# Two attention layers and an MLP on one core: loads, additions and one statistics operation placed in other slots

## The chip, the cores and the metric

The kernel runs on one core of a Trainium2 chip. The metric is the device time of one execution in microseconds (us), the median of several runs. Five engines work side by side: TensorE (PE, matmuls; its weight loads are PEld), VectorE (DVE), ScalarE (ACT), GpSimd (POOL) and SyncE (SP). SP computes nothing here; it issues DMAs, and ACT issues some too. Each engine runs its own list of instructions in the order in which the program wrote them, and waits at semaphores for the others.

## The reference, cut to what matters

The input x holds 16 batches of 256 tokens of 512 numbers; `ctx` has the same shape. All is float32, with 16 heads of 32.

```
ln = layernorm(x, ln1); q, k, v = split(ln @ w_qkv + b_qkv)
x = x + attention(q, k, v, ltor_mask) @ w_ao + b_ao          # first layer
ln = layernorm(x, ln2); q = ln @ w_q + b_q
k, v = split(ctx @ w_kv + b_kv)
x = x + attention(q, k, v, cross_mask) @ w_co + b_co         # second layer
x = x + gelu(layernorm(x, ln3) @ w1 + b1) @ w2 + b2          # MLP
# then a block of three small 1x1 convolutions of x and ctx, and their products, added to x

attention: scores = q k^T / sqrt(32); scores = scores * mask - 10000 * (1 - mask)
           softmax over the last axis, then times v
```

The products run in split precision: an operand is written as a high and a low part (names that end in `_h` and `_l`), and a product is three matmuls (lines L66, L67 and L68).

## The kernel before, in words

**Bodies and slots.** Two batches (512 tokens, four tiles of 128) are one block. The two attention layers are 16 bodies, k = 0 to 15: bodies 0 to 7 are the first layer over the eight blocks, bodies 8 to 15 the second. In a body the kernel works on block r and lets the work of its neighbours overlap: it prepares x and the contexts of the next block, and finishes the output product of the block before (k - 1). Each body has eight slots, h = 0 to 7. Each slot handles one group of four heads of one batch at each stage of a pipeline: the scores of one group, the maxima and exponentials of the group before it, the turns (transposes) and the product with v of a still older one. In the same slot TensorE has two units of a projection: q and k in slots 0 to 3, v in slots 4 and 6, and in slots 5 and 7 the output product of the block before, whose tiles are o0, o1 (slot 5) and o2, o3 (slot 7).

**What a slot needs from each engine.** TensorE: the units (L66 to L68), the scores (L1052), the product with v (L1086), the turns (L1068). VectorE: the masked scores (L1655, 128x1024, two of them, called mask here), the row maxima (L1665, eight, each with two inputs in SBUF), the low part of q or k (L1638), or for an output tile the sum of the product in PSUM and the residual (L1633); then the reciprocals (L1672) and their transpose (L1675), and the scaling of the product with v (L1693). ScalarE: exponentials (L1306), copies of the turned exponentials (L1367), the high parts. GpSimd: the low part of the weighed product (L817), the halves of the contexts (L805, L810), and the addition of the output bias to each residual tile (`add_bias`, L776, two SBUF inputs, 128x512).

**Two trips through DRAM.** The reciprocals go from `A_turned_inv` to `inverses` in DRAM and come back as `A_rt` (issued by SP, L533 and L543), and VectorE needs them at L1693. The exponentials go out (L555) and come back turned as `A_pt` (L565), which TensorE needs at L1086.

**Residual tiles.** The tile buffers `res[0]` and `res[1]` serve o0, o1 and then o2, o3. Tile t is loaded from `x` (function `load_res` of ScalarE's queue, slot 2 for tiles 0 and 1, slot 6 for tiles 2 and 3), gets its bias from GpSimd (slot 4; slot 7), is added to the product by VectorE (slot 5; slot 7), and is stored by SP (`store`, L503).

**Other work that the change touches.** `chunks` are pieces of the second layer's weights (128x512), loaded into `wst` by SP in bodies 7 and 8 (`load_chunk`, L490) and split into high and low part by the other engines (`split_chunk`). The loads of the contexts of the next block are in ScalarE's queue. `row_statistics` (VectorE, L1603) takes the batch statistics of a tile of x for the next layer norm: two tiles in slot 0, two in slot 1. In body 15 GpSimd also normalises rows for the MLP (L909 to L914).

The order on every engine is the order in which the program writes it: nothing is planned at run time. Where an instruction waits, all behind it on that engine wait too.

Of the kernel before, what the change touches and what calls it, by code (L numbers as in the profile page):

```python
# [11 lines left out]
P = 128  # L12
# [125 lines left out]
def whole_network(nc, ctx, nl, m1t_dram, inv_dram, p_dram, xt_dram, rows, x1, x2, ctx_t, s_mask, x_mask, s_weights, x_weights, fold_wt, columns,  # L138
# [20 lines left out]
    KEPT = range(GROUPS - 12, GROUPS)  # L159

    with ExitStack() as stack:
# [150 lines left out]
        chunk_at = {(7, 4): (0, 1, 2), (7, 5): (3, 4), (7, 6): (5,), (7, 7): (6, 7)}  # L312
        chunk_at.update({(8, 0): (8,), (8, 1): (9,), (8, 2): (10, 11)})
        chunk_at.update({(9, n): (12 + n,) for n in range(4)})
        load_at = {(7, 0): (0, 1), (7, 3): (2, 3), (7, 4): (4, 5), (7, 6): (6, 7), (7, 7): (8,), (8, 0): (9,), (8, 1): (10, 11),
# [14 lines left out]
        ld_x, ld_e = room.sems("ld_x", TT), room.sems("ld_e", BPB)  # L330
        ld_r, st_y, ld_m = room.sems("ld_r", 2), room.sems("st_y", 2), room.sems("ld_m", BPB)
# [149 lines left out]
        def _(sp):  # L481
            def load_chunk(n):
                c, t = chunks[n]
                if n < KT:
                    sp.wait_ge(folded, 4 * KT)
                elif chunks[n - KT][0] == 0:
                    sp.wait_ge(w_lo, 4 * KT + chunks[n - KT][1] + 1)
                else:
                    sp.wait_ge(w_lo2, sum(1 for c_, _ in chunks[:n - KT + 1] if c_))
                sp.dma_start(wst[:, n % KT, :], x_weights[c][t * P:(t + 1) * P, :]).then_inc(ld_s[n % KT], DMA)  # L490
# [131 lines left out]
            def slot(r, k, h, a_, b_, own, pv):  # L622
# [135 lines left out]
        def _(pool):  # L758
# [94 lines left out]
            def slot(r, k, h, a_, b_, own, pv):  # L853
# [3 lines left out]
                if h == 7 and k < NU:  # L857
                    if k:
# [18 lines left out]
                if h == (4 if 1 < k < NU else 1) and k:  # L877
# [381 lines left out]
        def _(act):  # L1259
# [303 lines left out]
        def _(dve):  # L1563
# [60 lines left out]
            def unit_out(item, r, k):  # L1624
# [148 lines left out]
            def slot(r, k, h, a_, b_, own, pv):  # L1773
# [40 lines left out]
                if k < NU and h in ((0, 1) if k else (1, 2)):  # L1814
                    row_statistics(r + 1, 0 if h == (0 if k else 1) else 2)
# [189 lines left out]
```

## Time and profile before

| | |
|---|---|
| median of three runs | 2012.24 us (2012.05 to 2014.52) |
| the profiled execution | 2015.01 us |
| its span in the trace | 2013.2 us |
| TensorE busy | 1976.3 us (98%) |
| VectorE busy | 1476.2 us (73%) |
| ScalarE busy | 1161.6 us (58%) |
| GpSimd busy | 547.1 us (27%) |
| granted TensorE clock | 0.998 of full speed |

Bodies 0 to 15 end at about 1235 us of the span, and the rest is MLP and the last block, which the change doesn't touch. The page says "busy" for a matmul with a modelled end, so a gap on TensorE looks a little shorter than the delay it stands for. A row of a timeline is: start, duration, engine, line, operation, tiles, count; in square brackets how long the engine had been idle before, and who released it. The waits view sums these gaps by line and by releaser.

### The profile page before, as it was taken

How to read it: one execution, taken by the hardware profiler on the slowest of the kernel's cores; microseconds unless marked ns; L12 is line 12 of the kernel's file. 1: busy time of each engine (PE TensorE's matmuls, PEld its weight loads, DVE VectorE, ACT ScalarE, POOL GpSimd, SP SyncE). 2: the span in 40 equal slices, each digit the busy share in tenths (PEclk: the TensorE clock that was granted, in tenths of full speed). 3: DMA queues.
4: the chain of work that ended last, by engine and by line, in shares of the span. 5: the costliest groups of instructions: out<-in, count | busy, mean ns of one | idle time of the engine just before them, and what ended most of it. 6: DMA issues, size and time to landing. Idle time of an engine off the chain costs nothing. (4 is left out here: it accounts for less than half of the span.)

```text
span 2013.2 us, 41550 instructions
## 1 busy us (share of the span) xinstructions
PE 1976.3 (98%) x13632; PEld 1569.7 (78%) x13632; DVE 1476.2 (73%) x3868; ACT 1161.6 (58%) x3251; POOL 547.1 (27%) x556
## 2 busy tenths in 40 slices
PE   9999999999999999999999998999999999999998
PEld 8977777777776777777777776888888888888887
DVE  7799999999998999899899889564444443435333
ACT  4388888888888888888888888521212111212111
POOL 1012222222224334323423432053132131313000
PEclk9999999999999999999999999999999999999999
DMA  8546667667667877767867734541212212121201
GB/s 273 173 94 139 147 165 158 129 162 163 135 176 184 194 171 171 172 160 172 184 150 166 187 92 116 171 107 35 79 40 69 68 47 78 47 63 51 62 24 48
DMA packets 681720, 252.67 MB, mean 126 GB/s; under 512 B 533312, under 2 KB 626112, under 8 KB 681536
## 3 DMA queue, kind: packets, MB, share of 16 engines
q1 hardware_dynamic: 533600, 192.16, 38.1%
q10 hardware_dynamic: 147936, 58.22, 12.0%
q8 instruction: 95, 1.56, 0.3%
q14 instruction: 89, 0.73, 0.1%
HBM read 167.41 MB, written 82.84 MB: 124 GB/s over the span
## 5 line engine op out<-in xcount | busy, mean ns | idle before, releaser
L1306 ACT ACTIVATE A_p<-A_p,A_nmax 128x256 f32<-128x256 f32 x1024 | 507.1, 501 | 3.5 <-DVE A_res L1633 1.7
L1665 DVE CUSTOM_DVE_ANT_0 A_p<-A_p,A_ma 128x256 f32<-128x256 f32 x1024 | 377.1, 423 | 4.6
L1655 DVE TENSOR_TENSOR A_p<-A_sc,A_mk 128x1024 f32<-128x1024 f32 x256 | 312.1, 1219 | 50.8 <-PE A_tp L1068 50.2
L817 POOL TENSOR_TENSOR A_ct_l<-A_cx,A_ct_h 128x256 fp32r<-128x256 f32 x122 | 114.2, 936 | 653.0 <-DVE A_nmax L1665 639.5
L1367 ACT ACTIVATE A_pt<-A_tp 128x512 f32<-128x512 f32 x396 | 218.2, 588 | 51.4 <-PE A_tp L1068 50.2
L1068 PEld LDWEIGHTS A_tp<-A_ident,A_p 128*128 128x128 f32 x1584 | 179.4, 141 | 72.6 <-ACT A_p L1306 35.4
L1068 PE MATMUL A_tp<-A_ident,A_p 128*128 128x128 f32 x1584 | 223.1, 278 | 2.9 <-ACT A_pt L1367 2.1
L1504 ACT ACTIVATE A_mk<-A_tp,A_cols 128x512 f32<-128x512 f32 x62 | 42.7, 689 | 269.0 <-PE A_tp L68 269.0
L1306 ACT ACTIVATION_READ_ACCUMULATOR A_p<-A_p,A_nmax 128x1 f32 x1024 | 197.4, 193 | 0.0
L1504 ACT ACTIVATE A_ma<-A_tp,A_cols 128x512 f32<-128x512 f32 x62 | 42.8, 690 | 242.1 <-PE A_tp L68 242.1
L66 PE MATMUL A_banks<-A_xt_h,A_w_h 128*128 128x512 f32 x384 | 162.0, 422 | 3.3 <-DVE A_res L1633 2.3
L1856 DVE CAST A_h_h<-A_ma 128x512 fp32r<-128x512 f32 x64 | 33.5, 524 | 161.8 <-ACT A_ma L1504 158.1
L68 PE MATMUL A_banks<-A_xt_h,A_w_l 128*128 128x512 f32 x384 | 151.1, 394 | 0.0
L926 POOL TENSOR_TENSOR A_v<-A_v,A_b_row 128x512 f32<-128x512 f32 x32 | 51.3, 1624 | 365.2 <-DMA A_v<-x 365.2
L67 PE MATMUL A_banks<-A_xt_l,A_w_h 128*128 128x512 f32 x384 | 150.2, 391 | 0.0
L1374 ACT ACTIVATE A_cx<-A_cx,A_bias_sum 128x256 f32<-128x256 f32 x128 | 65.2, 509 | 140.4 <-DVE A_cx L1693 140.2
L66 PE MATMUL A_tp<-A_xt_h,A_w_h 128*128 128x512 f32 x368 | 143.4, 390 | 0.3 <-DVE A_xt_l L1870 0.3
L67 PE MATMUL A_tp<-A_xt_l,A_w_h 128*128 128x512 f32 x368 | 143.2, 389 | 0.0
L68 PE MATMUL A_tp<-A_xt_h,A_w_l 128*128 128x512 f32 x368 | 143.2, 389 | 0.0
L1086 PE MATMUL A_banks<-A_pt,A_v 128*32 128x256 f32 x2048 | 137.9, 387 | 4.5 <-DMA A_pt<-exponentials 2.2
L1856 DVE CAST A_h_h<-A_mk 128x512 fp32r<-128x512 f32 x64 | 30.0, 468 | 143.0 <-ACT A_mk L1504 140.8
L66 PE MATMUL A_banks<-A_w_h,A_ct_h 128*128 128x512 f32 x256 | 105.9, 414 | 1.6 <-issue 1.1
(248 smaller groups left out, 4997.2 us busy)
## 6 DMA issues: line engine op xcount, KB each, us to landing
exponentials<-A_ln_shift SPq DMA_DIRECT2D x464, 64.0 KB, 2.7
A_pt<-exponentials SPq DMA_DIRECT2D x116, 256.0 KB, 3.1
A_rt<-inverses SPq DMA_DIRECT2D x512, 32.0 KB, 2.6
x<-A_res SPq DMA_DIRECT2D x64, 256.0 KB, 3.6
A_res<-x ACTq DMA_DIRECT2D x58, 256.0 KB, 4.3
turned<-A_x ACTq DMA_DIRECT2D x224, 64.0 KB, 2.7
A_x<-x ACTq DMA_DIRECT2D x56, 256.0 KB, 3.3
A_x<-x SPq DMA_DIRECT2D x40, 256.0 KB, 3.2
```

Of the source, the lines that this page charges most:

```text
L66: pe.matmul(out, sh, mh, start=first, stop=False)
L67: pe.matmul(out, sh, ml, start=False, stop=False)
L68: return pe.matmul(out, sl, mh, start=False, stop=last)
L817: pool.tensor_tensor(ct_l[:, f, part], cx[:, :], f32(ct_h[:, f, part]), ALU.subtract).then_inc(c_lo, 1)
L1068: last = pe.transpose(tp[:, n % 2, c * S + t * P:c * S + (t + 1) * P], p[:, g % 2, j, t, c * P:(c + 1) * P], ident[:, :])
L1086: last = pe.matmul(banks[rr, bank, 0:S], v[:, b * TPB + c, f * P + j * HD:f * P + (j + 1) * HD], turned_keys(grp, j, c), start=(c == 0), s ...
L1306: act.activation(p[:, g % 2, j, t, :], p[:, g % 2, j, t, :], ACT.Exp, scale=-1.0, bias=nmax[:, g % 2, j, t:t + 1], accum_out=rsum[:, g % 2 ...
L1367: act.activation(pt[:, moved(grp) + i, :, :], tp[:, n % 2, :].rearrange("p (c s) -> p c s", c=TPB), ACT.Copy)\
L1374: act.activation(cx[:, :], cx[:, :], ACT.Identity, bias=bias_sum[:, layer(k, h, -2), 2, f:f + 1]).then_inc(c_sum, 1)
L1504: act.activation(hf[f % 4], hidden_bank(blk, f), ACT.Gelu_apprx_tanh, bias=b1_col[:, f:f + 1])\
L1655: dve.tensor_tensor(p[:, g % 2, heads, :, :].rearrange("p j t s -> p j (t s)"), sc[:, heads, :], m, ALU.mult)\
L1665: dve.tensor_tensor_reduce(out=a_, in0=a_, in1=ma[:, b, t, :], scale=-1.0, scalar=BIG, op0=ALU.add, op1=ALU.min, accum_out=nmax[:, g % 2, ...
```

## The change

Five edits, none of which changes what is computed.

1. **Contexts.** For the bodies 8 to 14 the loads of the next block's two contexts (512 KB each) move on ScalarE's queue from slots 2 and 3 to slots 1 and 2. Body 7 has them there already.
2. **Body 15's first additions.** Residual tiles 0 and 1 are loaded in slot 0 in place of slot 2, and GpSimd adds their bias in slot 1 in place of slot 4.
3. **Chunks.** In body 7 the loads of chunks 4 and 5 move on SP from slot 4 to slot 5, and chunk 4 is split in slot 6 with chunk 5, no longer in slot 5 with chunk 3.
4. **A statistics operation.** The statistics of tile 0 move from slot 0 to the end of slot 7 of the body before, behind the sum for o3. So that its x is there, the load of this tile moves from ScalarE's queue (slot 6) to SP's (slot 5).
5. **Two more residual tiles.** In the bodies of `FOUR` (4, 5, 6, 10, 11, 12, 13) tiles 2 and 3 live in `wst[2]` and `wst[3]`, which are free there. They are loaded on ScalarE's queue in slot 3 in place of slot 6, and GpSimd adds both biases in slot 5 in place of slot 7.

```
-        chunk_at = {(7, 4): (0, 1, 2), (7, 5): (3, 4), (7, 6): (5,), (7, 7): (6, 7)}
+        chunk_at = {(7, 4): (0, 1, 2), (7, 5): (3,), (7, 6): (4, 5), (7, 7): (6, 7)}
-        load_at = {(7, 0): (0, 1), (7, 3): (2, 3), (7, 4): (4, 5), (7, 6): (6, 7), ...
+        load_at = {(7, 0): (0, 1), (7, 3): (2, 3), (7, 5): (4, 5), (7, 6): (6, 7), ...
+        def res_tile(k, t):
+            return wst[:, t, :] if four(k, t) else res[:, t % 2, :]
+        def four(k, t):
+            return k + 1 in FOUR and t > 1
...
 SP, load_chunk:
+                    for half_ in range(2):
+                        sp.wait_ge(st_y[half_], (7 - 1) * 2 * DMA)
 SP, slot:
+                if by_blocks(k) and h == 5:
+                    sp.wait_ge(st_a[0], (turned_before(k, r) + 1) * TPB * (P // 32) * DMA)
+                    sp.dma_start(x[:, 0, :], row_tile(0, k + 2, r + 2, 0)).then_inc(ld_x[0], DMA)
...
 GpSimd, slot:
                 if h == 7 and k < NU:
-                    if k:
+                    if k and k not in FOUR:
                         add_bias(k - 1, r - 1, 2)
                         until_first_maxima(r, h)
                         add_bias(k - 1, r - 1, 3)
-                if h == (4 if 1 < k < NU else 1) and k:
+                if h == (4 if 1 < k < NU - 1 else 1) and k:
                     add_bias(k - 1, r - 1, 0)
                     add_bias(k - 1, r - 1, 1)
+                if h == 5 and k in FOUR:
+                    add_bias(k - 1, r - 1, 2)
+                    add_bias(k - 1, r - 1, 3)
...
 ScalarE, loads:
-                if by_blocks(k) and (h, n) == (6, 3):
-                    load_row(k + 2, r + 2, 0)
-                if NB <= k + 1 < NU and n == 4 and h in ((1, 2) if k + 1 == NB else (2, 3)):
-                    load_context(r + 1, h - (1 if k + 1 == NB else 2))
+                if NB <= k + 1 < NU and n == 4 and h in (1, 2):
+                    load_context(r + 1, h - 1)
-                if 1 < k < NU and h == 2 and n in (5, 6):
+                if 1 < k < NU and h == (2 if k < NU - 1 else 0) and n in (5, 6):
                     load_res(k - 1, r - 1, n - 5)
-                if 0 < k < NU and h == 6 and n in (5, 6):
-                    load_res(k - 1, r - 1, n - 3)
+                if 0 < k < NU and h == (3 if k in FOUR else 6) and n in ((3, 4) if k in FOUR else (5, 6)):
+                    load_res(k - 1, r - 1, n - (1 if k in FOUR else 3))
...
 VectorE, slot:
-                    row_statistics(r + 1, 0 if h == (0 if k else 1) else 2)
+                    if h != 0 or k < 2:
+                        row_statistics(r + 1, 0 if h == (0 if k else 1) else 2)
...
+                if by_blocks(k) and h == 7:
+                    row_statistics(r + 2, 0)
```

TensorE's own list of instructions stays as it is. Three places of the lists that change are shown here; the names are those of the tiles, written `output<-inputs`.

GpSimd, body 10, slots 4 to 7, before. `A_et_h` and `A_et_l` are the two parts of a context, `A_ct_l` is the low part of the weighed product, which waits for the maxima of its slot:

```order
L776 TENSOR_TENSOR A_res<-A_res,A_o_bias 128x512 x2
L817 TENSOR_TENSOR A_ct_l<-A_cx,A_ct_h 128x256
L805 CAST A_et_h<-A_e 128x4x128
L810 TENSOR_TENSOR A_et_l<-A_e,A_et_h 128x4x128
L805 CAST A_et_h<-A_e 128x4x128
L810 TENSOR_TENSOR A_et_l<-A_e,A_et_h 128x4x128
L805 CAST A_et_h<-A_e 128x4x128
L817 TENSOR_TENSOR A_ct_l<-A_cx,A_ct_h 128x256
L810 TENSOR_TENSOR A_et_l<-A_e,A_et_h 128x4x128
L776 TENSOR_TENSOR A_res<-A_res,A_o_bias 128x512 x2
```

The same place after:

```order
L797 TENSOR_TENSOR A_res<-A_res,A_o_bias 128x512 x2
L838 TENSOR_TENSOR A_ct_l<-A_cx,A_ct_h 128x256
L826 CAST A_et_h<-A_e 128x4x128
L831 TENSOR_TENSOR A_et_l<-A_e,A_et_h 128x4x128
L826 CAST A_et_h<-A_e 128x4x128
L831 TENSOR_TENSOR A_et_l<-A_e,A_et_h 128x4x128
L797 TENSOR_TENSOR A_wst<-A_wst,A_o_bias 128x512 x2
L826 CAST A_et_h<-A_e 128x4x128
L838 TENSOR_TENSOR A_ct_l<-A_cx,A_ct_h 128x256
L831 TENSOR_TENSOR A_et_l<-A_e,A_et_h 128x4x128
```

These rows (with the renumbered lines L817 to L838, L805 to L826, L810 to L831) show that the second pair of additions has moved from behind the third context half to directly behind the second.

SP, body 7, slots 4 to 6, before:

```order
L490 DMA A_wst<-L_xattn_w_q 128x512
L490 DMA A_wst<-L_xattn_w_kv 128x512
L565 DMA A_pt<-exponentials 128x4x128
L533 DMA inverses<-A_turned_inv 128x32
L555 DMA exponentials<-A_ln_shift 32x16x32 x4
L543 DMA A_rt<-inverses 32x4x64 x4
L731 DMA A_e<-turned 128x4x256
L503 DMA x<-A_res 128x512 x2
```

The same place after:

```order
L583 DMA A_pt<-exponentials 128x4x128
L551 DMA inverses<-A_turned_inv 128x32
L573 DMA exponentials<-A_ln_shift 32x16x32 x4
L561 DMA A_rt<-inverses 32x4x64 x4
L752 DMA A_e<-turned 128x4x256
L508 DMA A_wst<-L_xattn_w_q 128x512
L508 DMA A_wst<-L_xattn_w_kv 128x512
L687 DMA A_x<-x 128x512
L521 DMA x<-A_res 128x512 x2
```

The two chunk loads went from ahead of the slot's trips through DRAM to behind them, and the load of x's tile 0 stands behind them, ahead of the stores; this last load stands at that place in bodies 1 to 14.

The third place is on VectorE, at the end of slot 7 and in slot 0 of the next body. Before, in slot 0, both statistics stand in front of the low part of k:

```order
L1665 ISA A_nmax 128x1
L1603 BN_STATS A_stats<-A_x 128x6 x2
L1638 SCALAR_TENSOR_TENSOR A_k_l<-A_banks,A_bias_sum,A_k_h 128x512
L1655 TENSOR_TENSOR A_p<-A_sc,A_mk 128x1024
L1672 RECIPROCAL A_rinv<-A_rsum 128x8
```

After, from the end of the body before:

```order
L1644 TENSOR_TENSOR A_xt_l<-A_e,A_xt_h 128x4x256
L1655 TENSOR_TENSOR A_res<-A_banks,A_res 128x512
L1625 BN_STATS A_stats<-A_x 128x6
L1677 TENSOR_TENSOR A_p<-A_sc,A_mk 128x1024
L1694 RECIPROCAL A_rinv<-A_rsum 128x8
```

and in slot 0 itself:

```order
L1687 ISA A_nmax 128x1
L1625 BN_STATS A_stats<-A_x 128x6
L1660 SCALAR_TENSOR_TENSOR A_k_l<-A_banks,A_bias_sum,A_k_h 128x512
L1677 TENSOR_TENSOR A_p<-A_sc,A_mk 128x1024
L1694 RECIPROCAL A_rinv<-A_rsum 128x8
```

One of the two statistics stands in front of the low part of k where two stood, and the other stands ahead of the body's first mask.

## Rows read from the trace of the kernel before

**Rows 1.** The page: busy us of each engine, share, instructions.

```profile
PE 1976.3 (98%) x13632; PEld 1569.7 (78%) x13632; DVE 1476.2 (73%) x3868; ACT 1161.6 (58%) x3251; POOL 547.1 (27%) x556
```

**Rows 2.** Waits of TensorE, 140 to 651 us: total, times, longest.

```profile
PE A_banks L1086 <- DMA A_pt<-exponentials: 2.2, 3, 1.3
PE A_banks L66 <- DVE A_res L1633: 1.4, 4, 0.5
```

**Rows 3.** Waits of TensorE, 651 to 1161 us.

```profile
PE A_banks L66 <- DVE A_k_l L1638: 5.1, 8, 0.8
PE A_banks L66 <- DVE A_res L1633: 0.8, 3, 0.5
```

**Rows 4.** Timeline, VectorE and TensorE, body 9, slot 3.

```profile
748.15 0.42 DVE L1693 TENSOR_TENSOR A_cx<-A_banks,A_rt 128x256 f32<-128x256 f32 x1 [0.98 <-DMA A_rt<-inverses]
...
751.82 0.39 PE L1052 MATMUL A_sc<-A_k_h,A_q_h 32*128 32x256 f32 x4
...
752.74 1.07 PE L1086 MATMUL A_banks<-A_pt,A_v 128*32 128x256 f32 x16
...
755.62 0.50 PE L66 MATMUL A_banks<-A_w_h,A_et_h 128*128 128x512 f32 x1 [0.79 <-DVE A_k_l L1638]
```

**Rows 5.** Timeline, VectorE and TensorE, slot 7 of body 5 and what follows it.

```profile
488.11 0.42 DVE L1693 TENSOR_TENSOR A_cx<-A_banks,A_rt 128x256 f32<-128x256 f32 x1 [0.77 <-DMA A_rt<-inverses]
...
495.42 0.50 PE L66 MATMUL A_banks<-A_xt_h,A_w_h 128*128 128x512 f32 x1 [0.53 <-DVE A_res L1633]
```

**Rows 6.** Timeline, VectorE and TensorE, slot 0 of bodies 7 and 8.

```profile
574.72 1.29 DVE L1603 BATCH_NORM_STATS2 A_stats<-A_x 128x6 f32<-128x512 f32 x2
...
576.71 0.50 PE L66 MATMUL A_banks<-A_xt_h,A_w_h 128*128 128x512 f32 x1 [0.35 <-DVE A_k_l L1638]
...
655.06 0.50 PE L66 MATMUL A_banks<-A_xt_h,A_w_h 128*128 128x512 f32 x1 [0.55 <-DVE A_k_l L1638]
```

**Rows 7.** Timeline, SP's queue and TensorE, body 7, slots 4 and 5.

```profile
613.11 0.35 SPq L490 DMA_DIRECT2D A_wst<-L_xattn_w_q  x1
617.90 0.35 SPq L490 DMA_DIRECT2D A_wst<-L_xattn_w_kv  x1
618.35 0.38 SPq L565 DMA_DIRECT2D A_pt<-exponentials  x1
...
622.75 1.94 PE L1086 MATMUL A_banks<-A_pt,A_v 128*32 128x256 f32 x16 [1.29 <-DMA A_pt<-exponentials]
```

**Rows 8.** Timeline, body 15: GpSimd in its slot 4, VectorE and TensorE in slot 5.

```profile
1200.60 2.98 POOL L776 TENSOR_TENSOR A_res<-A_res,A_o_bias 128x512 f32<-128x512 f32 x2
...
1204.41 1.38 POOL L912 TENSOR_TENSOR A_x<-A_x,A_o_bias 128x512 f32<-128x512 f32 x1
...
1204.57 1.51 DVE L1665 CUSTOM_DVE_ANT_0 A_p<-A_p,A_ma 128x256 f32<-128x256 f32 x1
...
1209.15 0.39 PE L1052 MATMUL A_sc<-A_k_h,A_q_h 32*128 32x256 f32 x4 [0.92 <-DVE A_p L1655]
...
1213.04 0.50 PE L66 MATMUL A_banks<-A_w_h,A_et_h 128*128 128x512 f32 x1 [0.89 <-DVE A_res L1633]
```

**Rows 9.** Timeline, body 10: GpSimd in its slot 5, VectorE and TensorE in slot 6.

```profile
848.21 1.29 POOL L810 TENSOR_TENSOR A_et_l<-A_e,A_et_h 128x512 fp32r<-128x512 f32 x1
...
849.15 0.64 DVE L1665 CUSTOM_DVE_ANT_0 A_p<-A_p,A_ma 128x256 f32<-128x256 f32 x1
...
849.72 0.41 DVE L1665 CUSTOM_DVE_ANT_0 A_p<-A_p,A_ma 128x256 f32<-128x256 f32 x1
...
850.76 1.21 DVE L1655 TENSOR_TENSOR A_p<-A_sc,A_mk 128x1024 f32<-128x1024 f32 x1
...
852.82 0.39 PE L1052 MATMUL A_sc<-A_k_h,A_q_h 32*128 32x256 f32 x4
...
855.58 0.48 PE L66 MATMUL A_banks<-A_w_h,A_ct_h 128*128 128x512 f32 x1
```

**Rows 10.** Windows, body 9, slots 5 and 6: busy us by engine, clock, DMA share, GB/s.

```profile
772.60:778.60 6.00, 6.00 (x37) 5.09 (x34) 5.13 (x14) 4.26 (x11) 4.12 (x5) 1.00 1.01 254
```

More of the change, by code:

```diff
@@ L159, in whole_network @@
     KEPT = range(GROUPS - 12, GROUPS)
+    FOUR = (4, 5, 6, 10, 11, 12, 13)
     with ExitStack() as stack:
@@ L311, in whole_network @@
         chunks = [(0, 0), (1, 0), (0, 1), (0, 2), (0, 3), (1, 1), (1, 2), (1, 3)] + [(2, t) for t in range(KT)] + [(3, t) for t in range(KT)]
-        chunk_at = {(7, 4): (0, 1, 2), (7, 5): (3, 4), (7, 6): (5,), (7, 7): (6, 7)}
+        chunk_at = {(7, 4): (0, 1, 2), (7, 5): (3,), (7, 6): (4, 5), (7, 7): (6, 7)}
         chunk_at.update({(8, 0): (8,), (8, 1): (9,), (8, 2): (10, 11)})
         chunk_at.update({(9, n): (12 + n,) for n in range(4)})
-        load_at = {(7, 0): (0, 1), (7, 3): (2, 3), (7, 4): (4, 5), (7, 6): (6, 7), (7, 7): (8,), (8, 0): (9,), (8, 1): (10, 11),
+        load_at = {(7, 0): (0, 1), (7, 3): (2, 3), (7, 5): (4, 5), (7, 6): (6, 7), (7, 7): (8,), (8, 0): (9,), (8, 1): (10, 11),
                    (8, 2): (12,), (8, 3): (13, 14, 15)}
@@ L330, in whole_network @@
         ld_x, ld_e = room.sems("ld_x", TT), room.sems("ld_e", BPB)
+        ld_r4 = room.sems("ld_r4_", 2)
         ld_r, st_y, ld_m = room.sems("ld_r", 2), room.sems("st_y", 2), room.sems("ld_m", BPB)
@@ L431, in raw_pair, with res_loaded @@
             return e[:, n, :, :] if k < NB else f32(xt_l[:, :, 2 * n * P:(2 * n + 2) * P])
+        def res_tile(k, t):
+            return wst[:, t, :] if four(k, t) else res[:, t % 2, :]
+        def four(k, t):
+            return k + 1 in FOUR and t > 1
+        def res_loaded(k, t):
+            if four(k, t):
+                return ld_r4[t % 2], sum(four(m, t) for m in range(k + 1)) * DMA
+            return ld_r[t % 2], (sum(2 - four(m, 2) for m in range(k)) + t // 2 + 1) * DMA
         def late(k, h):
@@ L498, in load_res @@
                 wait(sp, st_y[t % 2], (r * 2 + t // 2) * DMA)
-                sp.dma_start(res[:, t % 2, :], row_tile(0, k, r, t)).then_inc(ld_r[t % 2], DMA)
+                sp.dma_start(res[:, t % 2, :], row_tile(0, k, r, t)).then_inc(res_loaded(k, t)[0], DMA)
             def store(k, r, t):
                 sp.wait_ge(y_ok, r * TT + (t + 1))
-                sp.dma_start(row_tile(1, k, r, t), res[:, t % 2, :]).then_inc(st_y[t % 2], DMA)
+                sp.dma_start(row_tile(1, k, r, t), res_tile(k, t)).then_inc(st_y[t % 2], DMA)
             def load_m_chunk(n):
@@ L774, in add_bias @@
             def add_bias(k, r, t):
-                pool.wait_ge(ld_r[t % 2], (r * 2 + (t // 2 + 1)) * DMA)
-                pool.tensor_tensor(res[:, t % 2, :], res[:, t % 2, :], o_bias[:, int(k >= NB), :], ALU.add)\
+                pool.wait_ge(*res_loaded(k, t))
+                pool.tensor_tensor(res_tile(k, t), res_tile(k, t), o_bias[:, int(k >= NB), :], ALU.add)\
                     .then_inc(res_ok, 1)
@@ L1326, in load_res @@
             def load_res(k, r, t):
-                wait(act, st_y[t % 2], (r * 2 + t // 2) * DMA)
-                act.dma_start(res[:, t % 2, :], row_tile(0, k, r, t)).then_inc(ld_r[t % 2], DMA)
+                wait(act, st_y[t % 2], (r * 2 + (0 if four(k, t) else t // 2)) * DMA)
+                act.dma_start(res_tile(k, t), row_tile(0, k, r, t)).then_inc(res_loaded(k, t)[0], DMA)
             def load_o_copy(t):
@@ L1632, in unit_out @@
                     dve.wait_ge(res_ok, (r - 1) * TT + (n + 1))
-                    dve.tensor_tensor(res[:, n % 2, :], o, res[:, n % 2, :], ALU.add).then_inc(y_ok, 1)
+                    dve.tensor_tensor(res_tile(k - 1, n), o, res_tile(k - 1, n), ALU.add).then_inc(y_ok, 1)
                 else:
```

## The prediction

> **What bounds the kernel now.** I read four views in this order. The page first: TensorE is busy 98% of the span [rows 1], so a move can only give back the few per cent of gaps in TensorE's row, or open new ones. Then TensorE's waits for the two attention layers [rows 2, 3]: they are a handful of small items, each with its releaser. Then the timeline at each item, upstream from TensorE to the engine that was late and to what made it late [rows 4 to 9]. Last a window for the DMA engines [rows 10].
>
> How a gap becomes time: in a slot without a wait, the next unit's first matmul starts 855.58 - 852.82 = 2.76 us after the scores [rows 9]. In body 9 it is 755.62 - 751.82 = 3.80, so the delay is 1.04 where the bracket says 0.79 [rows 4]. I add 0.25 to each recorded gap. A body that waits nowhere takes about 8 slots of one length, so a delay on TensorE goes into the end one for one; nothing later makes it up.
>
> **The change part by part (gain positive).**
>
> *Body 7, chunks.* SP issues the load of chunk 4 at 613.11, then stands before chunk 5 until 617.90, which holds the load of `A_pt` behind it until 618.35. TensorE waits 1.29 for it, and the 16 small matmuls then take 1.94 in place of 1.07 [rows 7, 4]. With both chunk loads a slot later, behind that load, the sum is 1.29 + 0.25 + 0.87 = 2.4. Chunk 4's split moves beside chunk 5's, which could take some of it back: between 0.5 and 2.7. I take 2.4, as the wait is seen whole.
>
> *Statistics.* In slot 0 of bodies 7 and 8 the two operations take 1.29 ahead of the low part of k, and TensorE then waits 0.35 and 0.55 [rows 6]; as delays 0.60 and 0.80. One operation less there is 0.65: gain 0.6 + 0.65 = 1.2. The other bodies have room for it in slot 0. At the end of slot 7 it stands behind the sum for o3, so it can delay only the next mask. Bounds -0.5 to 1.4.
>
> *Body 15.* GpSimd's two residual additions in slot 4 push the row additions L912 and its successor to 1204.41, where VectorE's maxima run: one takes 1.51 [rows 8] where another takes 0.41 [rows 9], and the next one is met in the same way. TensorE then waits 0.92 for the mask and 0.89 for o1's sum [rows 8]: 1.17 + 1.14 = 2.3. In slot 1 the additions fall on work that they don't block, if their loads land in time; I take 2.1, bounds 1.0 and 2.3.
>
> The Trainium skill (SBUF — State Buffer, "Who interferes with whom") states that a VectorE instruction with two SBUF inputs and a GpSimd instruction that reads SBUF lock each other out for a whole instruction. By that rule the maximum waits for the addition's end, and the trace agrees (1.51 against 0.41).
>
> *Slot 7, layer 1.* `A_rt` comes late there: VectorE idles 0.77 for it in body 5 and TensorE 0.53 at the end [rows 5]. Four such waits are 1.4 recorded [rows 2], 2.4 as delays. Bodies 4 to 6 lose two tile loads and the x load from slot 6, bodies 1 to 3 the x load alone. I take all of body 5 but a little (0.7), a third of the other three (0.6), and 0.2 off for new loads in slot 3: 1.1, bounds 0 and 2.4.
>
> *Slot 7, layer 2, bodies 10 to 13.* Three waits of 0.8 together [rows 3] are 1.55 as delays, and a fourth body has some 0.3 below the resolution of that view. All four lose three loads from slot 6: gain 1.9, bounds 0.5 and 1.9.
>
> *The same bodies, the additions in slot 5.* This is the costly term. In layer 1 the two additions of slot 5 follow the weighed product at once and are over before the maxima begin. In bodies 10 to 13 two context splits come first. The second ends at 848.21 + 1.29 = 849.50, and the first maximum, begun at 849.15, takes 0.64 since it is held until then [rows 9]. Now two additions of 1.3 each follow directly, over the maxima at 849.72 and behind it. As in body 15, each addition holds one maximum for 1.51 - 0.41 = 1.1. The mask that followed at 850.76 and ended at 851.97 comes 2.2 later, and the scores at 852.82 have 0.85 of room [rows 9]: a delay of 1.35 in slot 6. Four bodies: -5.4. Bounds: 0 (the additions slip between the maxima, which the 0.64 of the first one would allow) and 4 x 2.2 = 8.8 (the room is used up by something else). I take 5.4, as rows 8 show the same pair of operations.
>
> *Contexts.* One slot earlier they run beside x's tile load, two slots later beside two residual loads as before. In slot 3 of bodies 8 to 14 TensorE waits for k's low part, because `A_rt` comes 0.98 late behind one context and two residual tiles [rows 4]; eight waits of 5.1 are listed [rows 3]. The second context stays in slot 2 with both tiles, so these stay. Slot 1 takes 0.75 MB in place of slot 2's 1.0 MB, so I expect the trip there to be just in time: -0.5 for all seven bodies, bounds 0 and 7 x 1.04 = -7.3.
>
> *The x load on SP* stands behind the slot's trips through DRAM and ahead of two stores of the same size; nothing waits for these soon. In the slots 5 and 6 the DMA engines are full, 1.01 at 254 GB/s [rows 10], and the next `A_pt` and `inverses` are queued behind. I take -0.3 for it in all, with a rival below.
>
> The Trainium skill (DMA: Bandwidth & Descriptors, "Issuing engines are not separate DMA queues") says that DMAs started by different engines run on the same 16 and interleave. By it, moving x's load from ScalarE's queue to SP's saves no transfer time: what this term gives must come from the slot alone. Rows 10 show the crowd but not the origin of each packet.
>
> Sum: 2.4 + 1.2 + 2.1 + 1.1 + 1.9 - 5.4 - 0.5 - 0.3 = 2.5. The profiled execution took 2015.01 us, 2.8 above the median of 2012.24; the terms are differences and hold for either. Median: 2009.7, profiled execution about 2012.5.
>
> **The rivals.**
>
> *No collision.* The additions fall between the maxima, or the mask's room takes them up: 5.4 comes back, 2004.3. For it: the first maximum loses 0.23 only today [rows 9]. Against: additions back to back leave no gap, and rows 8 have two maxima held in a row.
>
> *Slower by the contexts.* If the context in slot 1 makes `A_rt` as late as in rows 4, slot 2 of bodies 8 to 14 gets a delay of 1.04 each: -7.3 in place of -0.5, 2016.5. It decides from the point where the trip lands more than about 0.4 after VectorE asks for it. For it: rows 4. Against: a quarter less to move than there, and body 7 has its contexts so placed and lists no such wait of its own in rows 2.
>
> *Slower by x's load.* At 254 GB/s its 256 KB are 1.03 us of full engines [rows 10]. If that falls on the trip for slot 7, the seven bodies with a wait there (4 + 3 in rows 2, 3) lose 1.03 each and the other seven half of it: 10.8. Without the two gains of slot 7 (3.0) and the -0.3: 2009.7 + 3.0 - 0.3 + 10.8 = 2023.2. Against it: the same 256 KB leave slot 6 at once, and in seven bodies 512 KB more.
>
> *Body 7 only shifts its stall.* The splits of chunks 4 and 5 together delay the mask of slot 6 as the missing load did: 1.9 less, 2011.6.
>
> **How the numbers follow.** A measurement of this kernel can tell about 0.2%, 4.0 us, from no change: faster is below 2008.2, slower above 2016.3. Chances: the forecast 0.56, with its own range 2006.5 to 2012.5, and 0.30 of it below 2008.2; no collision 0.20, nearly all faster; contexts 0.09, somewhat over half slower; x's load 0.05, slower; body 7 0.10, same. That gives faster 0.17 + 0.19 = 0.36, slower 0.05 + 0.05 + 0.01 = 0.11, same 0.53. The range leaves out the lower part of "no collision", x's load and the worse half of the contexts: 2002.8 to 2015.0.
>
> **What would show it.** In the changed kernel: in slot 6 of bodies 10 to 13 two maxima of some 1.5 us beside the `A_wst` additions, and a gap on TensorE before the scores, released by VectorE's mask, about 1.1 recorded. If these maxima stay near 0.4, the costly term is wrong. In body 7 no SP wait before `A_pt` and no gap before its product; if a gap before the scores of slot 6 or 7 of the same size is there, the stall has moved. The waits on `A_res` at the bodies' ends gone for 5 and 10 to 13, smaller for 1 to 3. Body 15 without its two gaps. The eight waits for k's low part after slot 3 still there, those of bodies 7 and 8 after slot 0 gone. New gaps after slot 2 in bodies 8 to 14, or `A_rt` waits on VectorE in slots 6 and 7, would speak for the slower rivals.

## The result, and the profile after

| | before | after |
|---|---|---|
| median (12 runs each) | 2012.14 us | 2017.26 us |
| range | 2007.87 to 2014.52 | 2014.00 to 2019.77 |
| ratio | | 1.0027, 95% interval 1.0020 to 1.0034 |
| profiled execution | 2015.01 us | 2018.07 us |
| span | 2013.2 us | 2016.2 us |

The change made the kernel slower by 0.27%, some 5.4 us, where 2.5 us of gain was forecast. The time lies outside the forecast's range. VectorE's busy time rose by 5.6 us, though it runs the same operations; the page of the changed kernel [rows 1 before]:

```profile
span 2016.2 us, 41547 instructions
PE 1977.5 (98%) x13632; PEld 1570.7 (78%) x13632; DVE 1481.8 (73%) x3868; ACT 1161.6 (58%) x3251; POOL 550.1 (27%) x556
```

TensorE's waits from 651 to 1161 us, the stretch of [rows 3], as total, times and longest:

```profile
PE A_sc L1076 <- DVE A_p L1677: 7.5, 5, 1.9
PE A_banks L66 <- DVE A_k_l L1660: 2.2, 5, 0.7
PE A_banks L66 <- DVE A_res L1655: 0.2, 1, 0.2
```

The waits on `A_res` at the ends of the bodies shrank as forecast. In their place TensorE waits for VectorE's mask (L1677, L1655 before): four waits of 1.8 to 1.9 us and a small one. Body 10, in the order GpSimd, VectorE, TensorE; it answers to [rows 9] (columns: start, duration, engine, line, operation):

```profile
845.09 1.29 POOL L831 TENSOR_TENSOR A_et_l<-A_e,A_et_h 128x512 fp32r<-128x512 f32 x1
846.33 2.93 POOL L797 TENSOR_TENSOR A_wst<-A_wst,A_o_bias 128x512 f32<-128x512 f32 x2
849.20 0.81 POOL L826 CAST A_et_h<-A_e 128x512 fp32r<-128x512 f32 x1
...
846.02 0.64 DVE L1687 CUSTOM_DVE_ANT_0 A_p<-A_p,A_ma 128x256 f32<-128x256 f32 x1
...
846.59 1.51 DVE L1687 CUSTOM_DVE_ANT_0 A_p<-A_p,A_ma 128x256 f32<-128x256 f32 x1
...
848.03 1.51 DVE L1687 CUSTOM_DVE_ANT_0 A_p<-A_p,A_ma 128x256 f32<-128x256 f32 x1
...
849.47 0.82 DVE L1687 CUSTOM_DVE_ANT_0 A_p<-A_p,A_ma 128x256 f32<-128x256 f32 x1
...
850.22 1.21 DVE L1677 TENSOR_TENSOR A_p<-A_sc,A_mk 128x1024 f32<-128x1024 f32 x1
...
851.58 0.39 PE L1076 MATMUL A_sc<-A_k_h,A_q_h 32*128 32x256 f32 x4 [1.82 <-DVE A_p L1677]
```

All four maxima are held: the first by the split (0.64, as before), two by the additions, and the fourth by the cast that follows them. The mask starts 4.20 us after the first maximum, where it was 850.76 - 849.15 = 1.61 before [rows 9]: 2.6 us more. The room before the scores takes 0.7 of it.

A second thing stands behind the gap. After it the product with v and the turns take their usual time in body 11, and nearly twice that in body 12. TensorE's timeline, body 12:

```profile
1000.75 1.91 PE L1110 MATMUL A_banks<-A_pt,A_v 128*32 128x256 f32 x16
1002.59 1.87 PE L1092 MATMUL A_tp<-A_ident,A_p 128*128 128x128 f32 x8
```

and body 11:

```profile
926.90 1.07 PE L1110 MATMUL A_banks<-A_pt,A_v 128*32 128x256 f32 x16
927.90 1.09 PE L1092 MATMUL A_tp<-A_ident,A_p 128*128 128x128 f32 x8
```

The windows view of the same two places (columns: busy us of the five engines, granted clock, DMA share, GB/s):

```profile
1001.00:1004.30 3.30, 3.30 (x25) 2.13 (x17) 1.90 (x4) 0.60 (x2) 2.86 (x3) 0.51 0.59 187
927.00:930.00 3.00, 3.00 (x30) 2.20 (x31) 2.91 (x7) 1.29 (x4) 2.41 (x2) 1.00 0.73 191
```

In body 12 the granted clock was 0.51, the lower of the two levels (1.2 GHz), right after an idle time of 1.83 us. I call this the half clock; it costs 1.62 us more. In this trace it happened in bodies 12 and 13 and not in 10 and 11, though all four gaps were 1.82 to 1.85 us.

In body 7 the wait for `A_pt` moved. SP's queue and TensorE in slots 5 and 6, to be read beside [rows 7]:

```profile
622.85 0.50 SPq L508 DMA_DIRECT2D A_wst<-L_xattn_w_q  x1
623.40 0.43 SPq L508 DMA_DIRECT2D A_wst<-L_xattn_w_kv  x1
623.87 0.43 SPq L687 DMA_DIRECT2D A_x<-x  x1
624.34 0.92 SPq L521 DMA_DIRECT2D x<-A_res  x2
625.66 0.37 SPq L583 DMA_DIRECT2D A_pt<-exponentials  x1
...
633.30 1.07 PE L1110 MATMUL A_banks<-A_pt,A_v 128*32 128x256 f32 x16 [1.97 <-DMA A_pt<-exponentials]
```

Five transfers of 256 KB stand ahead of it, and TensorE waits 1.97 us for it, here with no half clock behind it (the 16 matmuls take 1.07). Body 15 has neither of its gaps any more ([rows 8]; between 1161 and 1232 us the waits view lists nothing).

**Where the 3.1 us between the two spans are.** I compared the distance from each slot's scores to the next in both traces. What a distance has above that of a slot without a wait (8.9 us) is called the slot's delay.

| place | change, us | forecast |
|---|---|---|
| bodies 10 to 13, delay before the scores of slot 6 | +7.6 (4 x 1.90) | +5.4 |
| bodies 12 and 13, half clock behind it | +3.2 | none |
| bodies 10 to 13, slot 7 | -1.65 | -1.9 |
| body 7, slots 5 to 7 | -1.4 (-2.80 and +1.41) | -2.4 |
| bodies 7 and 8, slot 0 | -1.1 | -1.2 |
| body 15 | -1.9 | -2.1 |
| bodies 1 to 6, slots 6 and 7 | +1.2 | -1.1 |
| bodies 8 to 14, slots 2 and 3 | -3.8 | +0.5 |
| rest (bodies 8, 9, 14 and small ones) | +0.9 | +0.3 |

The eighth row is no effect of the change. These two slots have 7.4 us of delay in the profiled execution before and 3.6 to 5.1 in each of the 17 other traces of this study, also where nothing of them was edited. That execution was 2.9 us above its own median. A term of one or two us read from one execution has this much luck in it.

The fourth row has luck in it too. The 2.80 us of slot 5 hold a stretch at half clock behind the wait of 1.29 us [rows 7]. In s1, s2 and s4 (below), where edit 3 is absent too, the same wait is 1.02 to 1.11 us, the matmuls behind it take their usual time, and the delay of the slot is 1.1 to 1.2. From s1:

```profile
621.54 1.07 PE L1086 MATMUL A_banks<-A_pt,A_v 128*32 128x256 f32 x16 [1.09 <-DMA A_pt<-exponentials]
```

Slots 5 and 6 of body 7 have to be read together, since these traces have a wait of 1.70 to 1.86 us in slot 6: their delay is 3.4 before, 2.9 in s1, 3.0 in s4, 4.5 in s2 with half clock, 1.0 in s3 and 2.0 in the changed kernel.

### The profile page after: what moved, and what is told of

The parts are those of the page before. It is cut to its first block and busy times, and to the rows that moved or that the text cites. A ratio compares the mean times of both kernels' runs of the same rounds, so it can differ in the third digit from the quotient of the medians.

```text
span 2016.2 us, 41547 instructions
## 1 busy us (share of the span) xinstructions
PE 1977.5 (98%) x13632; PEld 1570.7 (78%) x13632; DVE 1481.8 (73%) x3868; ACT 1161.6 (58%) x3251; POOL 550.1 (27%) x556
## 5 line engine op out<-in xcount | busy, mean ns | idle before, releaser
L1687 DVE CUSTOM_DVE_ANT_0 A_p<-A_p,A_ma 128x256 f32<-128x256 f32 x1024 | 385.3, 431 | 4.6
L1677 DVE TENSOR_TENSOR A_p<-A_sc,A_mk 128x1024 f32<-128x1024 f32 x256 | 312.1, 1219 | 49.8 <-PE A_tp L1092 48.1
L838 POOL TENSOR_TENSOR A_ct_l<-A_cx,A_ct_h 128x256 fp32r<-128x256 f32 x122 | 114.4, 938 | 681.1 <-DVE A_nmax L1687 667.6
```

The costliest lines, as they stand in the source:

```text
L838: pool.tensor_tensor(ct_l[:, f, part], cx[:, :], f32(ct_h[:, f, part]), ALU.subtract).then_inc(c_lo, 1)
L1677: dve.tensor_tensor(p[:, g % 2, heads, :, :].rearrange("p j t s -> p j (t s)"), sc[:, heads, :], m, ALU.mult)\
L1687: dve.tensor_tensor_reduce(out=a_, in0=a_, in1=ma[:, b, t, :], scale=-1.0, scalar=BIG, op0=ALU.add, op1=ALU.min, accum_out=nmax[:, g % 2, ...
```

## The experiments

All ratios are to the kernel before on the same chip. The first eight ran beside a kernel before of 2011.4 and 2011.6 us. Three theories stood at the start: A, VectorE's maxima and GpSimd's instructions exclude each other, and the clock falls behind the gap; B, the transfers moved in SP's queue and into other slots cost the time everywhere; D, GpSimd's writes or the late context half behind the additions, not the reads, are at fault.

**The additions of bodies 10 to 13.**

e1, only bodies 4, 5 and 6 keep their tiles 2 and 3 in `wst`:

```
-    FOUR = (4, 5, 6, 10, 11, 12, 13)
+    FOUR = (4, 5, 6)
```

> The changed kernel with FOUR = (4, 5, 6): the bodies 10 to 13 load and add their residual tiles 2 and 3 as before, in slots 6 and 7. Theory A (shared port, then clock): the four delays of 1.90 us before the scores of slot 6 go, 7.6 us, and with them the two stretches of 1.62 us at half clock behind them, 3.2 us; the waits at the ends of these bodies come back, 1.7 us. From 2017.3: 2008.2, and about 0.2% below the kernel before. Rival B (the x load in SP's queue and the additional traffic in slots 5 and 6 cost the time everywhere): at most a quarter of the loss goes, 2015 to 2017.

Measured: 2007.47 us, ratio 0.9981 (0.9972 to 0.9990). As theory A expected (2008.2), and against B. All the loss and more hangs on bodies 10 to 13.

e2, the loads stay in slot 3 and only the additions go back to slot 7:

```
-                    if k and k not in FOUR:
+                    if k and (k not in FOUR or k >= NB):
...
-                if h == 5 and k in FOUR:
+                if h == 5 and k in FOUR and k < NB:
```

> The changed kernel, but in bodies 10 to 13 GpSimd adds the bias of residual tiles 2 and 3 in slot 7, where the kernel before does; the tiles are still loaded in slot 3 into wst. Theory A: it is the place of the additions that costs, not their loads: no gap before the scores of slot 6, maxima of 0.4 us there, and the ends of the bodies keep their gain: 2017.3 - 7.6 - 3.2 = 2006.5. Rival B: 2015 to 2017. Rival C (the loads in slot 3 delay the trip through DRAM for slot 4): a wait of VectorE for A_rt in slot 4 of these bodies, 2009 or more.

Measured: 2007.33 us, ratio 0.9984 (0.9976 to 0.9993). The gap before the scores is gone: TensorE's waits of this kernel from 797 to 1100 us begin with

```profile
PE A_banks L66 <- DVE A_k_l L1660: 1.3, 3, 0.8
PE A_banks L66 <- DVE A_wst L1655: 0.6, 2, 0.3
```

It is the place of two additions per body that costs, not the loads. The medians of e1 and e2 are 0.14 us apart and their intervals overlap, so the early loads in bodies 10 to 13 give nothing that can be measured here. The expectation that the ends of these bodies keep their gain did not come true: the delay in slot 7 of the four is 1.9 before, 2.2 in e1, 1.6 in e2 and 0.3 in the changed kernel, so most of the gain there comes with the early additions.

e3, fills in place of the additions:

```
+                if four(k, t) and k >= NB:
+                    pool.memset(res_tile(k, t), 0.0).then_inc(res_ok, 1)
+                    return
```

> The changed kernel, but in bodies 10 to 13 the two additions of slot 5 are two fills of the same tiles by GpSimd, which read nothing (the residual and bias of these tiles are left out of the result). Theory A in its sharp form, that VectorE's maxima and GpSimd's reads of SBUF exclude each other: the maxima beside the fills take 0.4 us, the gap before the scores goes, 2006.5. Rival D (it is GpSimd's writes as well, or the late context half behind the additions): maxima of over 1 us as before, and 2012 to 2017.

Measured: 2006.87 us, ratio 0.9977 (0.9968 to 0.9985). GpSimd and VectorE in body 10:

```profile
843.57 1.29 POOL L834 TENSOR_TENSOR A_et_l<-A_e,A_et_h 128x512 fp32r<-128x512 f32 x1
844.79 0.99 POOL L798 MEMSET A_wst<- 128x512 f32 x2
...
844.49 0.65 DVE L1690 CUSTOM_DVE_ANT_0 A_p<-A_p,A_ma 128x256 f32<-128x256 f32 x1
...
845.07 0.42 DVE L1690 CUSTOM_DVE_ANT_0 A_p<-A_p,A_ma 128x256 f32<-128x256 f32 x1
...
845.41 0.42 DVE L1690 CUSTOM_DVE_ANT_0 A_p<-A_p,A_ma 128x256 f32<-128x256 f32 x1
```

This kernel leaves out the residual and the bias of these tiles. The maximum at 845.07 and the next run beside the two fills at their usual 0.42. The fills are also shorter (0.99 us for both against 2.93), but an instruction that held the port would still have held the maximum that starts beside it. The Trainium skill (SBUF — State Buffer, "Who interferes with whom") says that a VectorE instruction with two SBUF inputs contends with a GpSimd instruction that reads SBUF, not with one that only writes it; the trace agrees.

e4, the same instructions with the additions ahead of the context splits:

> The changed kernel, but in bodies 10 to 13 the two additions of slot 5 stand ahead of the two context splits and not behind them. The same work for GpSimd, in another order. Theory A: the additions are over about 3.3 us after the weighed product's low part and before the maxima; what lies over the maxima now is the second half of the splits, a cast and an addition of the same size (0.6 and 1.3 us): one or two maxima held, so a delay of 0.3 to 1.1 us before the scores of slot 6 in place of 1.90, and no half clock behind it: 2017.3 - 10.8 + 2.8 = 2009.3. Rival B: 2015 to 2017.

Measured: 2014.71 us, ratio 1.0016 (1.0006 to 1.0026). A miss: 2009.3 was expected. VectorE in body 10, whose four maxima lie beside a split (1.29), a cast, a split and a cast of GpSimd:

```profile
843.35 1.21 DVE L1687 CUSTOM_DVE_ANT_0 A_p<-A_p,A_ma 128x256 f32<-128x256 f32 x1
...
844.49 0.82 DVE L1687 CUSTOM_DVE_ANT_0 A_p<-A_p,A_ma 128x256 f32<-128x256 f32 x1
...
845.24 1.50 DVE L1687 CUSTOM_DVE_ANT_0 A_p<-A_p,A_ma 128x256 f32<-128x256 f32 x1
...
846.67 0.82 DVE L1687 CUSTOM_DVE_ANT_0 A_p<-A_p,A_ma 128x256 f32<-128x256 f32 x1
```

I had counted how long GpSimd's work overlaps; what counts is how many of its instructions meet a maximum, since the two take turns. Each instruction, short or long, holds one maximum for about its own length. The gap was 1.7 us, and in the profiled execution the half clock followed it in three of the four bodies. In the medians there is less of it. e4 is 7.4 us above e2 on the same chip; its delays before the scores are 7.1, its ends of bodies 10 to 13 give back 1.3, and 1.7 is left.

**Dose.** g1 has one addition in slot 5 and the other in slot 7, g2 has three (g1's lines of slot 7 and the semaphore of g2's extra addition are left out here):

```
 g1:                 add_bias(k - 1, r - 1, 2)
+                    if k < NB:
                         add_bias(k - 1, r - 1, 3)
 g2:                 add_bias(k - 1, r - 1, 2)
+                    if k >= NB:
+                        pool.wait_ge(res_ok, (r - 1) * TT + 3)
+                        pool.tensor_tensor(res_tile(k - 1, 2), res_tile(k - 1, 2), o_bias[:, 1, :], ALU.add)
                     add_bias(k - 1, r - 1, 3)
```

> The changed kernel with one of the two additions of bodies 10 to 13 in slot 5, the other in slot 7. Each instruction of GpSimd holds one maximum: by the addition 1.1 us, by the cast behind it 0.4. The mask of slot 6 is 1.5 us later than without, has 0.85 - 0.15 of room, and the gap before the scores is 0.8 in place of 1.9; no half clock, since the gap is short. From 2017.3: 4 x 1.1 and 2 x 1.6 less, 2009.7. Rival: the two additions count together or not at all, 2007 or 2017.

> The changed kernel with a third addition of the same size between the two, in bodies 10 to 13 (one bias is added twice, so tile 2 is off in the result). Each addition holds one of the four maxima: three of 1.5 us, and the fourth is held by the cast: a gap of 3.0 us before the scores in place of 1.9. After such a gap the granted clock should be at half in all four bodies, where it was in two of four: +4 x 1.1 + 2 x 1.6 = 7.6, 2024.9. Rival: if the half clock has nothing to do with the length of the gap, it is there in the same share of bodies, 2021.7.

These ran on a chip where the kernel before took 2015.91 us. Measured: g1 2014.52 us, ratio 0.9991 (0.9982 to 1.0000); g2 2019.81 us, ratio 1.0022 (1.0013 to 1.0031). For g2 this is a miss: 2024.9 was expected, a ratio of 1.0063 to the 2012.1 of the result's chip, and its rival's 2021.7 (1.0048) is too high as well. The traces of the profiled executions:

| kernel | additions | delay before the scores, bodies 10 to 13 | half clock behind it |
|---|---|---|---|
| e2 | 0 | none | none |
| g1 | 1 | 1.20, 0.81, 0.83, 0.82 | 0 of 4 |
| e4 | 2, ahead | 1.75 to 1.80 | 3 of 4 |
| changed kernel | 2 | 1.89 to 1.92 | 2 of 4 |
| g2 | 3 | 2.56 to 2.58 | 4 of 4 |

The delay grows by 1.1 for the second addition, as forecast for g1, and by 0.66 for the third, not by 1.1: there are only four maxima, so the third addition takes the cast's turn. In bodies 11 to 13 of g1 the cast starts a little later, the third maximum takes 0.41 and the cast holds the fourth; in its body 10 the split holds the first for 1.04, which makes the 1.20. In g2 the clock is at the lower level behind the gap, here in body 12:

```profile
1005.60:1008.60 3.00, 3.00 (x28) 1.51 (x24) 1.75 (x5) 0.00 (x0) 2.25 (x2) 0.50 0.63 198
```

**One chip for the steps.** The steps above were measured on different chips, so the changed kernel, e2, b2 (below) and g2 were timed together, as r1 to r4.

> The changed kernel itself, on one chip with the three others. Theory A: above r2 by 4 x 1.90 = 7.6 plus 1.6 for each body with half clock; two of four in the first trace, so 10.8 us in a run like that one, 0.27% above the kernel before in the median.

> The additions of bodies 10 to 13 in slot 7, as e2. Theory A: 7.6 to 14 us below r1, by how many of the four bodies meet the half clock in r1. No gap before the scores of slot 6 in bodies 10 to 13 and no half clock there.

> Three additions in slot 5 of bodies 10 to 13, as g2. The gap before the scores is 2.5 us where r1 has 1.8: 4 x 0.66 = 2.6 above r1 if the half clock follows the gaps equally often, 2.6 + 1.6 for each body in which it comes now and did not in r1, at most 2.6 + 6.4. Its trace should have the half clock in at least three of the four bodies.

| | us | ratio |
|---|---|---|
| r1, the changed kernel | 2017.39 | 1.0027 (1.0017 to 1.0037) |
| r2, additions in slot 7 | 2007.21 | 0.9973 (0.9962 to 0.9983) |
| r4, three additions | 2019.74 | 1.0033 (1.0020 to 1.0046) |

r1 is 10.2 us above r2. Of this 7.6 are held maxima, and the ends of bodies 10 to 13 give 1.3 back (delay in slot 7: 0.3 in r1, 1.6 in r2). That leaves 3.9 for the half clock and all else, some two bodies of four. r1's trace again has it in bodies 12 and 13, r4's in all four. TensorE's waits, 651 to 1161 us, r1 and then r4:

```profile
PE A_sc L1076 <- DVE A_p L1677: 7.4, 4, 1.9
```

```profile
PE A_sc L1080 <- DVE A_p L1681: 10.2, 5, 2.5
```

But r4 is only 2.4 us above r1 in the medians, about the longer gaps alone (4 x 0.66), where its profiled execution is 7.5 above (2025.24 against 2017.79) and the slowest of its runs. The mean granted clock of every execution on record tells the same:

| kernels | executions | mean granted clock |
|---|---|---|
| e2 and r2, no addition in slot 5 | 19 | 0.9982 |
| g1 | 11 | 0.9983 |
| e4 | 12 | 0.9978 |
| the changed kernel and r1 | 20 | 0.9967 |
| g2 and r4, without their two profiled ones | 14 | 0.9972 |

The two profiled executions of g2 and r4 have 0.995. The others of these kernels have 0.995 to 0.999, and as a group no lower a clock than the changed kernel. With 0.999 an execution cannot have had what the profiled ones had, so half clock in all four bodies is not the rule behind gaps of 2.5 us. Between the changed kernel and e2 with r2 the difference of 0.0015 is, over 2010 us, an estimate of 3 us of full-speed time, near the 3.9 left above. The estimate counts TensorE's idle time as lost too, so it is rather too high than too low.

**The edits one by one, on the kernel before.**

> The kernel before with the first edit alone: the two contexts of bodies 8 to 14 one slot earlier. The prediction's account was -0.5 us of gain. Theory A: the trace of the changed kernel has 3.8 us less delay behind the scores of slots 2 and 3 in these bodies, and if the contexts do that, this kernel is 3.5 us faster, 2008.6, with the waits for the low part of k in 651 to 1161 us down from 5.1 to about 2.2. Rival B: the gain there is of the other edits (the residual loads in slot 3), and this one gives nothing: 2012, waits of 5 us.

> The kernel before with the second edit alone: body 15's first two residual loads in slot 0 and additions in slot 1. Both gaps on TensorE at 1209 and 1213 us go: 1.9 us (0.99 and 0.88 in the changed kernel's trace), 2010.2. Rival: the loads in slot 0 fall beside four large loads of slot 1, the additions come late and hold the maxima of slot 1: a new gap there of up to 1 us, 2011.5.

> The kernel before with the third edit alone: chunk loads 4 and 5 in slot 5 of body 7. Theory A: the wait for A_pt in slot 5 goes (2.8 us with the half clock behind it), and a part comes back in slot 6, because the next A_pt load now stands behind two chunk loads and two stores in SP's queue (256 KB each); without the load of x between them the part is smaller than the 1.4 us seen in the changed kernel: net gain 1.8, 2010.3. Rival B, as forecast: the gain is 2.4, 2009.7, with no wait for A_pt in slot 6. Rival C: the stall moves whole, 2012.

> The kernel before with the fourth edit alone: one statistics operation at the end of slot 7, and the load of its tile on SP in slot 5. Theory A: slot 0 of bodies 7 and 8 gives 1.1 us, and the x load in SP's queue ahead of the stores puts inverses and A_pt of slots 6 and 7 later, which gives some of it back at the ends of bodies: 2011 to 2013, no clear change. Rival B: with the x load out of slot 6 the ends of the bodies gain too, 1.1 + 1.1 us: 2010.0. Rival C: one us later everywhere, over 2016.

| edit alone | us (before: 2011.58) | ratio | what its trace shows |
|---|---|---|---|
| s1 contexts | 2011.78 | 1.0001 (0.9992 to 1.0009) | waits for k's low part 3.0 (651 to 1161 us); 3.0 and 3.8 in s2 and s3 too, so not its doing |
| s2 body 15 | 2010.32 | 0.9992 (0.9983 to 1.0001) | both gaps gone, -1.95 |
| s3 chunks | 2009.17 | 0.9988 (0.9979 to 0.9997) | body 7: -2.79 in slot 5, +0.37 in slot 6 (against the profiled execution before) |
| s4 statistics and x load | 2013.14 | 1.0006 (0.9997 to 1.0015) | five waits for `A_pt`, 4.4 in all |

Theory A for s1 was wrong and its rival right on the time: the contexts are neutral. Its waits of 5 us did not come: they are 3.0 to 3.8 in s1, s2 and s3 alike, so the 5.1 before [rows 3] was of that one execution. s3 gives the 2.4 us of the forecast in the median (interval 0.6 to 4.2), with a wait of 0.9 in slot 6 that the forecast did not have. With edit 4 that wait grows. TensorE's waits for `A_pt` from 140 to 651 us, s3 and then s4:

```profile
PE A_banks L1086 <- DMA A_pt<-exponentials: 0.9, 1, 0.9
```

```profile
PE A_banks L1089 <- DMA A_pt<-exponentials: 4.4, 5, 1.9
```

s4 has no edit 3, so two of its five waits are body 7's own (1.02 in slot 5, 1.86 in slot 6); before, three waits make 2.2 [rows 2].

**Versions without the loss.** b1 is e2 without edit 4. b2 is e2 with the x load in SP's slot 6, behind the `A_pt` load:

```
-                if by_blocks(k) and h == 5:
+                if by_blocks(k) and h == 6:
                     sp.wait_ge(st_a[0], ...)
                     sp.dma_start(x[:, 0, :], row_tile(0, k + 2, r + 2, 0)).then_inc(ld_x[0], DMA)
```

> All edits but the fourth (statistics operation and x load are as before), with the additions of bodies 10 to 13 in slot 7. If edit 4 costs what it cost alone (1.2 us, interval -0.6 to 3.0), this is 2006.1 where the same kernel with edit 4 took 2007.3. Rival: with the residual loads out of slot 6 the x load on SP costs nothing and the earlier statistics still give 1.1 us in bodies 7 and 8: 2008.4.

> All edits, additions of bodies 10 to 13 in slot 7, and SP loads tile 0 of x in slot 6 and not in slot 5: behind the load of A_pt, not ahead of it. Theory A (what edit 4 costs is the A_pt load and the inverses behind one transfer more in SP's queue): in body 7 the wait of TensorE for A_pt in slot 6 falls from about 1.9 to under 1.0 us and has no half clock behind it, time 2005.5. Rival: the wait moves to slot 7 of body 7 and of others, 2007 to 2008.

> As r2 with SP's load of x's tile 0 in slot 6, as b2. Theory A: body 7 has its A_pt wait in slot 6 at 1.0 us or less where r2 has 1.9 and, in part of the runs, half clock behind it: 1 to 2.5 us below r2. Rival: the same as r2 within 0.5 us.

Measured, on the chip of 2015.91: b1 2007.79, ratio 0.9958 (0.9945 to 0.9972); b2 2006.06, ratio 0.9954 (0.9941 to 0.9968). On r1's chip (2012.33): r3 2004.76, ratio 0.9961 (0.9948 to 0.9974), 2.4 us below r2. The intervals of r3 and r2 overlap, with five and seven runs, and those of b1 and b2 do too, so no gain of the moved load is clear of noise. In body 7 b2's `A_pt` load stands behind four transfers and not five:

```profile
629.40 1.07 PE L1110 MATMUL A_banks<-A_pt,A_v 128*32 128x256 f32 x16 [1.05 <-DMA A_pt<-exponentials]
```

The wait is 1.05 where it was 1.97, and the delay that comes back in slot 6 is 0.47 in place of 1.41. In e2 that wait was followed by the half clock too, and the delay was 2.9. b1's wait is 1.0 as well. Over all traces with edit 3 the wait in slot 6 is 1.40 to 2.03 us in the ten that have the x load ahead of it, and 0.94 to 1.15 in the four that don't (s3, b1, b2, r3). So the lengthening of this wait is shown. But b2's rival was half right, for b2 and r3 have a new wait in slot 7 (1.03 in r3); b2's:

```profile
639.28 1.07 PE L1110 MATMUL A_banks<-A_pt,A_v 128*32 128x256 f32 x16 [0.91 <-DMA A_pt<-exponentials]
```

Slots 5 to 7 of body 7 have a delay of 2.5 in b2 and 2.8 in the changed kernel, 2.3 in r3 and 2.7 in r2. Body 7 therefore does not explain 2.4 us between r2 and r3, whose profiled executions are only 0.5 apart; where the rest comes from, if it is more than noise, stays open. r3 is 12.6 us faster than the changed kernel on the same chip and has the lowest median of the study.

## Why the prediction was wrong, point by point

- *The additions in slot 5*, put at -5.4, is the step that failed, by size and not by mechanism. The forecast had the two maxima at 1.5 us, and they are there. It let two instructions hold two maxima (+2.2); the cast behind them holds one more (+0.4), and the 0.85 us of room is 0.7, since the scores begin 0.15 after the mask's end. So 1.90 per body and not 1.35: 7.6 us, 2.2 more than forecast.
- *What follows the gap* was a term put at nothing, and is the larger part of that step's error: 3.2 us in the trace, and 3 to 4 by r1 against r2. Together the term measured 10.8 in the trace. [rows 7] had it: the 16 matmuls at 1.94 behind the gap in body 7. I put these 0.87 us down to the body's own term and did not ask whether the new gaps, longer than that one, would bring the same. Why the clock falls behind some of these gaps and not behind others as long stays open.
- *The x load on SP* was given 0.3 us. By itself edit 4 cost 1.6 us (s4, not clear of zero), and r3 against r2 differ by 2.4 (not clear of zero either). Of the forecast's rivals this is the one named "slower by x's load", right in one place (the `A_pt` load of body 7) and far too large in its price (10.8). The ends of bodies 1 to 3 gained nothing by it.
- *Slot 7, layer 1*, was given +1.1. The delay in slots 6 and 7 of bodies 1 to 6 is 2.4 before and 3.6 in the changed kernel, but it varies: 1.1 to 2.6 in the four traces without edits there (before, s1, s2, s3), 1.2 to 3.6 in the ten with all of them, 1.4 and 1.6 in b2 and r3. No gain is seen while the x load stands in SP's slot 5.
- *Body 7* gave 2.4 alone and 1.4 with edit 4. 0.87 of the 2.4 rested on a stretch at half clock that s1 and s4 don't have. The forecast's rival that the stall moves was half right, but through the queue, not through the splits.
- *Body 15, slot 0 of bodies 7 and 8, slot 7 of bodies 10 to 13* came out within 0.3 us each. Body 15's gain is in every trace with edit 2. Slot 0 is partly luck: its delay is 1.5 before, but 0.7 to 1.2 in s1, s2 and s3, where nothing of it was edited, and 1.0 in s4.
- *Contexts*: neutral, within its bounds. The rival of 7 us is refuted: VectorE does not wait for `A_rt` in slot 2 of bodies 8 to 14, neither in s1 nor in the changed kernel. That its 2016.5 lies nearest to the measured time is chance.
- *Held maxima in rows 8*: the rows show one maximum at 1.51; the second, said to be met in the same way, is in the same trace at 1206.01 with 1.50, so that reading was right.

The range reached up to 2015.0. It did include the term's own bound of 8.8 for the additions, which gives 2013.1. With 10.8 for them and the rest of the sum as it stood the time would be 2015.1, and the smaller misses (body 7, slots 6 and 7 of the first layer) carry it over the edge.

## What to carry to other kernels

When GpSimd work is moved beside two-input VectorE work, count its instructions, casts included. Here each that reads SBUF held one maximum for about its own length, and the order in which GpSimd did them hardly mattered (delays of 1.75 to 1.80 in e4, 1.89 to 1.92 in the changed kernel). A gap of TensorE is to be priced with the slow matmuls that can stand behind it, as a chance and not as a certainty. In bodies 1 to 15 of these traces they came behind no gap of 1.15 us or less, behind the only one of 1.29 us, behind none of four of 1.40 to 1.60 us, and behind 19 of 29 of 1.68 us and more. And a load that nothing waits for can lengthen another's wait, if it is put ahead of it in the same queue.

## What the runs showed of the hardware

- The two engines took turns: with GpSimd's instructions back to back, in all eight bodies 10 to 13 of the two traces of the changed kernel each of four maxima was held by a different one (about 0.65, 1.51, 1.51 and 0.82 us against 0.42), and a fill of the same tile held none.
- In the bodies 10 to 13 of the profiled executions the granted clock stayed at 1.00 behind recorded gaps of TensorE of 0.74 to 1.13 us in 4 of 4 places; behind 1.69 to 1.85 us it fell to the lower level in 7 of 12; behind 2.5 in 8 of 8. It cost 1.35 to 1.62 us each time. In slot 6 of body 7 it fell behind 4 of 9 gaps of 1.68 to 2.03 us and behind none of 8 shorter ones (0.94 to 1.60), and in slot 5 behind the 1.29 us of the kernel before. Equal gaps differed in this, in both traces of the changed kernel it was the same two bodies, and the mean clocks of the other executions say that 8 of 8 is more than usual.
- The same kernel before took 2011.4, 2011.6, 2012.3 and 2015.9 us in the median on different chips, more than most of the terms weighed here.
